# A Mamba scan with a routed FFN on one core: eight softplus sums on TensorE, other small work divided anew between VectorE and GpSimd, and a shorter routing chain

## What is computed

```python
xn = layernorm(x)
# attention part: layernorm again, then two Mamba blocks, one forward, one on the reversed sequence
xi, z = split(xn2 @ in_w.T);  xi = silu(conv4(xi) + conv_b)          # 256 inner features
dt, B, C = split(xi @ x_w.T)                                          # 8, 16, 16
delta = softplus(dt @ dt_w.T + dt_b)
h[t] = h[t-1] * exp(delta[t] * A) + (delta[t] * xi[t]) * B[t]         # 256 x 16 states
y[t] = sum_n h[t] * C[t] + xi[t] * D;   out = (y * silu(z)) @ out_w.T
attn = concat(out_f, out_b) @ combine_w.T + combine_b + xn
# FFN part: each token goes to one of 8 experts, argmax of xn @ router_w.T
ffn = down(silu(gate(xn)) * up(xn)) of that expert
result = x + attn + ffn
```

## Time and profile before

| | before |
|---|---|
| time, median of 3 runs (lowest to highest) | 910.14 us (907.42 to 910.88) |
| the profiled execution's own time | 907.48 us |
| its span, first to last instruction | 905.7 us |
| PE / DVE / ACT / POOL busy | 738.3 / 883.4 / 696.3 / 802.3 us |

### The profile page before, as it was taken

How to read it: one execution, slowest core, us unless ns; L and a number is a source line. 1 busy time by engine, 2 the same in 40 slices (tenths; PEclk the granted TensorE clock), 3 DMA queues, 4 the chain that set the end, 5 groups by cost and what they waited for, 6 DMA issues and landing times.

```text
span 905.7 us, 10749 instructions
## 1 busy us (share of the span) xinstructions
PE 738.3 (82%) x3033; PEld 329.6 (36%) x3033; DVE 883.4 (98%) x635; ACT 696.3 (77%) x1185; POOL 802.3 (89%) x453
## 2 busy tenths in 40 slices
PE   8889867886588988989797987989878879679376
PEld 5334312331134534444343533445333432224032
DVE  6999999999899999999999999999999999999997
ACT  5998864845479889988989989897979976575650
POOL 0788787999999999898899998999798999999996
PEclk8969797687799989999899999989989897988689
DMA  8894344134355555545455626455553444462400
GB/s 234 226 278 113 116 105 142 52 101 113 114 146 169 146 190 145 166 125 139 146 144 180 174 81 208 120 171 140 175 143 91 143 97 148 113 184 61 108 0 13
DMA packets 90988, 123.60 MB, mean 136 GB/s; under 512 B 7977, under 2 KB 63274, under 8 KB 86962
## 3 DMA queue, kind: packets, MB, share of 16 engines
q1 hardware_dynamic: 88882, 118.72, 46.5%
q0 software_dynamic: 2048, 4.20, 1.5%
HBM read 75.57 MB, written 14.29 MB: 99 GB/s over the span
## 4 chain that ended last, share of the span: by engine, by line
issue 39%; POOL 30%; PE 13%; ACT 9%; DVE 6%; DMA 1%; SPq 0%; ACTq 0%; POOLq 0%; DVEq 0%
POOL hs L1485 19%; POOL sorted_tokens L1496 4%; ACT dA L1032 3%; POOL gu_w L1458 3%; DVE hs L1245 2%; PE in_b L626 2%; DVE in_b L1226 2%; PE y L660 2%; ACT L1041 2%; POOL tmpA L1418 2%; PE front L579 2%; PE front L619 2%; POOL du L1423 1%; DVE hs L1243 1%; POOL yg L1468 1%
## 5 line engine op out<-in xcount | busy, mean ns | idle before, releaser
L1485 POOL TENSOR_TENSOR hs<-hs,C_rep 128x1024 f32<-128x1024 f32 x250 | 585.4, 2362 | 45.8 <-DVE hs L1245 24.6
L1032 ACT ACTIVATE dA<-delta_rep,A_sb 128x511 f32<-128x511 f32 x512 | 335.3, 717 | 20.4 <-DMA delta_rep<-tmpA 16.3
L1226 DVE TENSOR_TENSOR in_b<-in_b,B_rep 128x1024 f32<-128x1024 f32 x256 | 301.2, 1225 | 3.3 <-PE in_b L626 2.1
L1245 DVE TENSOR_TENSOR_SCAN hs<-dA,in_b 128x1024 f32<-128x1024 f32 x128 | 286.0, 2276 | 5.4 <-PE y L660 5.1
L1243 DVE TENSOR_TENSOR_SCAN hs<-dA,in_b 128x1024 f32<-128x1024 f32 x128 | 285.6, 2274 | 0.9 <-PE y L660 0.9
L626 PE MATMUL in_b<-du,cst 128*128 128x512 f32 x256 | 162.4, 721 | 60.9 <-DVE hs L1245 43.7
L660 PE MATMUL y<-hs,cst 128*32 128x512 f32 x1016 | 136.4, 655 | 22.1 <-POOL hs L1485 22.1
L579 PE MATMUL front<-xpad,w_in 128*128 128x512 f32 x248 | 117.4, 608 | 7.2 <-ACT xi L961 5.6
L1041 ACT ACT_TABLE_LOAD x71 | 91.1, 1283 | 11.6 <-PE moe L809 7.1
L626 PEld LDWEIGHTS in_b<-du,cst 128*128 128x128 f32 x256 | 47.7, 216 | 134.4 <-issue 129.9
L579 PEld LDWEIGHTS front<-xpad,w_in 128*128 128x128 f32 x248 | 46.2, 195 | 63.2 <-issue 49.8
(11 more groups left out here) (166 smaller groups left out, 810.7 us busy)
## 6 DMA issues: line engine op xcount, KB each, us to landing
delta_rep<-tmpA SPq DMA_DIRECT2D x126, 256.0 KB, 3.9
C_rep<-dbc_scratch SPq DMA_DIRECT2D x16, 1024.0 KB, 7.3
B_rep<-dbc_scratch SPq DMA_DIRECT2D x15, 1024.0 KB, 5.2
gu_w<-in_gate_up SPq DMA_DIRECT2D x39, 384.0 KB, 3.8
dn_w<-in_down SPq DMA_DIRECT2D x39, 192.0 KB, 2.6
xs<-sorted_tokens SPq DMA_DIRECT2D x39, 64.0 KB, 3.9
sorted_ffn<-ys SPq DMA_DIRECT2D x39, 64.0 KB, 2.4
sorted_tokens<-up_f SPq DMA_DIRECT2D x9, 256.0 KB, 4.5
```

What stands on the lines that cost most here:

```text
L1032: i = e.activation(dA[:, m % NA, r * L + 1:(r + 1) * L], src, ACT.Exp, scale=A_sb[:, d, 2 * p + jj, RH * rh + r:RH * rh + r + 1])
L1226: e.tensor_tensor(to, in_b[:, 2 + 2 * odd, :].unsqueeze(1).broadcast_to([P, RH, L]), by, ALU.mult).then_inc(dve_mult, 1)
L1245: e.tensor_tensor_scan(to[:, ::-1], a[:, 1:n + 1][:, ::-1], b[:, ::-1], 0.0, ALU.mult, ALU.add).then_inc(dve_scan, 1)
L1485: e.tensor_tensor(hs[:, m % NH, :], hs[:, m % NH, :], C_rep[:, u % 2, RH * rh:RH * rh + RH, :].rearrange("p r t -> p (r t)"), ALU.mult).th ...
```

## The change

- `SUM_STEP` names eight half-units, (3,0), (3,1), (4,0), (4,1), (14,0), (14,1), (15,0), (15,1). Their sum relu + ln is made by PE with two matmuls by the identity into bank `M` (`sum_delta`), at steps 41, 43, 57, 59, 218, 219, 232 and 235, and copied to `tmpA` by ACT one step later (`keep_delta`). POOL's addition is dropped there. SP's first `load_pair` of units 3 and 15 comes three steps later.
- `DU_STEP`: for unit 3 DVE multiplies delta, read from `M`, by xi (`first_du`), at steps 42 and 44; POOL does neither.
- `GATE_ON_DVE` gains i = 27 and 28. `C_ON_DVE` loses 41, 56, 180, 217 and 226 and keeps only the last, 255.
- The routing scans the one-hot before the matmuls instead of the counts behind them; one more matmul takes the place of a copy, a subtraction and an addition on DVE, the tile-to-expert table has one tile a partition (128x8 elements in place of 39x8 on each), and parts are packed: 18 instructions in place of 21, `pos_u` ready at step 32 in place of 35. The scatters and the loads in front of them start two steps sooner (POOL from step 31, SP from step 30).
- The `final_mm` of batches 2, 4 and 5 and the first transpose of the tiles wait for the copies out of `M`.

```diff
-GATE_ON_DVE = (3, 4, 5, 2 * UNITS - 1)
-C_ON_DVE = (41, 56, 180, 217, 226, LAST - 1)
+GATE_ON_DVE = (3, 4, 5, 27, 28, 2 * UNITS - 1)
+C_ON_DVE = (LAST - 1,)
+DU_STEP = {(3, 0): 42, (3, 1): 44}
+SUM_STEP = {(3, 0): 41, (3, 1): 43, (4, 0): 57, (4, 1): 59,
+            (UNITS - 2, 0): 218, (UNITS - 2, 1): 219, (UNITS - 1, 0): 232, (UNITS - 1, 1): 235}
...
                 for v in fronts(m, -5, -8):
-                    load_pair(v, 0)
+                    if (v, 0) not in SUM_STEP or v % 2 == 0:
+                        load_pair(v, 0)
+                for v in fronts(m, -5, -5):
+                    if (v, 0) in SUM_STEP and v % 2:
+                        load_pair(v, 0)
...
-                    if R0 + 5 + 20 * c // 8 == m:
+                    if R0 + 3 + 20 * c // 8 == m:
...
+            def sum_delta(v, h):
+
+                e.wait_ge(act_log, 2 * v + h + 1)
+                if (v, h) == (3, 0):
+                    e.wait_ge(dve_route, N_POS)
+                elif (v, h) == (UNITS - 2, 0):
+                    e.wait_ge(act_fin, 2)
+                elif v == UNITS - 1:
+                    e.wait_ge(act_fin, 4 + h)
+                if sums_on_pe(v, h) > 1:
+                    e.wait_ge(act_delta, sums_on_pe(v, h) - 1)
+                if 1 < sums_on_pe(v, h) <= 1 + len(DU_STEP):
+                    e.wait_ge(dve_du, sums_on_pe(v, h))
+                e.matmul(M[:, :], ident, tmpA[:, h, :], start=True, stop=False)
+                e.matmul(M[:, :], ident, tmpB[:, h, :], start=False, stop=True).then_inc(pe_delta, 1)
...
+                if b == 2:
+                    e.wait_ge(act_delta, sums_on_pe(UNITS - 2, 1))
+                if b >= 4:
+                    e.wait_ge(act_delta, sums_on_pe(UNITS - 1, b - 4))
...
+                for v, h in SUM_STEP:
+                    if SUM_STEP[v, h] == m:
+                        sum_delta(v, h)
...
-                if m == R0 + 3:
+                if m == R0 + 2:
                     e.wait_ge(dve_route, N_ONE)
-                    e.matmul(M[:, 0:256], tri, scratch(0), start=True, stop=True)
-                    e.matmul(M[:, 256:512], ones[:, :], scratch(0), start=True, stop=True).then_inc(pe_route, 1)
+                    upto = scratch(1)
+                    e.matmul(M[:, 256:256 + E], ones[:, :], upto[:, NBLK - 1::NBLK], start=True, stop=True)
+                    e.matmul(M[:, 0:256], ones[:, :], upto, start=True, stop=False)
+                    e.matmul(M[:, 0:256], tri, scratch(0), start=False, stop=True).then_inc(pe_route, 1)
...
+            def keep_delta(v, h):
+                e.wait_ge(pe_delta, sums_on_pe(v, h))
+                e.copy(tmpA[:, h, :], M[:, :]).then_inc(act_delta, 1)
...
+                for v, h in SUM_STEP:
+                    if SUM_STEP[v, h] + 1 == m:
+                        keep_delta(v, h)
...
+            def first_du(v, h):
+
+                wait_delta(e, v, h)
+                e.wait_ge(act_xi, 2 * v + h + 1)
+                e.wait_ge(pe_du, J * (v - 1 - h) + 4 + 4 * h)
+                e.tensor_tensor(du[:, du_slot(v, h), :], M[:, :], xi[:, v % 2, h, :], ALU.mult).then_inc(dve_du, 1)
...
+                elif part == 3:
+                    e.wait_ge(dve_route, 5)
+                    e.tensor_tensor_scan(upto, notfirst, one, 0.0, ALU.mult, ALU.add).then_inc(dve_route, 1)
...
-                elif part == 7:
-                    e.wait_ge(pe_route, 1)
-                    e.tensor_copy(val, M[:, 256:512]).then_inc(dve_route, 1)
...
-                    e.tensor_tensor(
-                        te.rearrange("p (n e) -> p n e", e=E), end_p.unsqueeze(1).broadcast_to([P, NTILE, E]),
-                        cst[:, C_TILE:C_TILE + NTILE].unsqueeze(2).broadcast_to([P, NTILE, E]),
-                        ALU.is_le).then_inc(dve_route, 1)
...
+                    e.tensor_scalar(te, end_p, cst[:, C_TILE:C_TILE + 1], None, ALU.is_le).then_inc(dve_route, 1)
...
             def delta_du(v, h):
-                e.wait_ge(act_log, 2 * v + h + 1)
-                e.tensor_tensor(tmpA[:, h, :], tmpA[:, h, :], tmpB[:, h, :], ALU.add).then_inc(pool_delta, 1)
+                if (v, h) not in SUM_STEP:
+                    e.wait_ge(act_log, 2 * v + h + 1)
+                    e.tensor_tensor(tmpA[:, h, :], tmpA[:, h, :], tmpB[:, h, :], ALU.add).then_inc(pool_delta, 1)
...
-                        if R0 + 6 + (20 * c + 5 * k) // 8 == m:
+                        if R0 + 4 + (20 * c + 5 * k) // 8 == m:
```

More of the change, by code:

```diff
@@ L134, in c_on_dve, with sums_on_pe, du_on_dve, du_on_pool @@
     return sum(x <= m for x in C_ON_DVE)
+def sums_on_pe(v, h):
+    return sum(k <= (v, h) for k in SUM_STEP)
+def du_on_dve(v, h):
+    return 1 + sum(k <= (v, h) for k in DU_STEP)
+def du_on_pool(v, h):
+    return 2 * v + h + 1 - du_on_dve(v, h)
+def sums_on_pool(v, h):
+    return 2 * v + h - sums_on_pe(v, h)
 def mamba_moe_kernel(nc, x, in_wT, conv_wT, x_wT, dt_wT, A_log, out_w, comb_wT, comb_b,
@@ L319, in wait_du @@
         def wait_du(e, v, h):
-            if v == 0 and h == 0:
-                e.wait_ge(dve_du, 1)
+            if v == 0 and h == 0 or (v, h) in DU_STEP:
+                e.wait_ge(dve_du, du_on_dve(v, h))
             else:
-                e.wait_ge(pool_du, 2 * v + h)
+                e.wait_ge(pool_du, du_on_pool(v, h))
         def wait_gated(e, i):
@@ L1273, in route @@
             def route(part):
-                one, val, pref, tmp = (scratch(i) for i in range(4))
-                rank, cum = M[:, 0:256], M[:, 256:512]
-                ntile, end_p, first, end = M[:, 0:E], M[:, E:2 * E], M[:, 2 * E:3 * E], small[:, 0:E]
-                te = th_f[:, :, :].rearrange("p a c -> p (a c)")[:, 0:NTILE * E]
+                one, upto, pos, tmp = (scratch(i) for i in range(4))
+                rank, notfirst = M[:, 0:256], M[:, 256:512]
+                total, ntile = M[:, 256:256 + E], M[:, 256 + E:256 + 2 * E]
+                first, end_p = small[:, E:2 * E], M[:, 256 + 2 * E:256 + 3 * E]
                 ke, ek = "p (k e) -> p k e", "p (e k) -> p e k"
-                best, low = small[:, 0:32], small[:, 32:64]
+                best, low, end, te = small[:, 0:32], small[:, 32:64], small[:, 0:E], tmp[:, E:2 * E]
                 if part == 0:
@@ L1310, in route @@
                     e.wait_ge(dve_route, 8)
[L1311 to L1314 removed]
+                    e.tensor_tensor_scan(end, ones[:, 0:E], ntile, 0.0, ALU.mult, ALU.add).then_inc(dve_route, 1)
                     e.wait_ge(dve_route, 9)
[L1316 to L1322 removed]
@@ L1323, in route @@
                     e.tensor_tensor(first, end, ntile, ALU.subtract).then_inc(dve_route, 1)
                     e.tensor_copy(end_p, end).then_inc(dve_route, 1)
[L1325 to L1326 removed]
+                elif part == 8:
+                    e.wait_ge(dve_route, 11)
                     e.scalar_tensor_tensor(
[L1328 to L1347 removed]
@@ new lines, in route @@
+                        rank.rearrange(ek, e=E), first.unsqueeze(2).broadcast_to([P, E, NBLK]), float(P),
+                        rank.rearrange(ek, e=E), ALU.mult, ALU.add).then_inc(dve_route, 1)
+                    e.wait_ge(dve_route, 12)
+                    e.tensor_tensor(pos, rank, one, ALU.mult).then_inc(dve_route, 1)
+                elif part == 9:
+                    e.wait_ge(dve_route, 13)
+                    e.tensor_reduce(low, pos.rearrange("p (e k) -> p k e", e=E), AX_X, ALU.add).then_inc(dve_route, 1)
+                    e.tensor_scalar(te, end_p, cst[:, C_TILE:C_TILE + 1], None, ALU.is_le).then_inc(dve_route, 1)
+                elif part == 10:
+                    e.wait_ge(dve_route, 15)
+                    e.tensor_copy(pos_u[:, :], low).then_inc(dve_route, 1)
+                    e.tensor_reduce(tmp[:, 0:1], te, AX_X, ALU.add).then_inc(dve_route, 1)
+                elif part == 11:
+                    e.wait_ge(dve_route, 17)
+                    e.tensor_scalar(ej_i[:, :], tmp[:, 0:1], float(E - 1), None, ALU.min).then_inc(dve_route, 1)
@@ L1397, in vector_program @@
                         gate(i)
+                for v, h in DU_STEP:
+                    if DU_STEP[v, h] == m:
+                        first_du(v, h)
                 if m == LAST + 5:
@@ L1478, in gpsimd_program @@
                     for v in fronts(m, (-7, -4)[h], (-8, -6)[h]):
-                        delta_du(v, h)
+                        if (v, h) not in DU_STEP:
+                            delta_du(v, h)
                 if m < LAST and m not in C_ON_DVE:
@@ L1513, in shape_constants @@
     c[:, C_ID:C_ID + P] = np.eye(P)
-    c[:, C_TRI:C_TRI + P] = np.triu(np.ones((P, P)), 1)
+    c[:, C_TRI:C_TRI + P] = np.triu(np.ones((P, P)), 1) - 1.0
     c[:, C_SEL:C_SEL + DD] = np.repeat(np.eye(DD), G, axis=0)
```

73 lines of the change are left out of this document (25 added, 48 removed).

## The result

| | before | after |
|---|---|---|
| median (lowest to highest, runs) | 910.51 us (907.42 to 913.84, 4) | 900.59 us (896.49 to 901.36, 4) |
| ratio, 95% interval | | 0.9882 [0.9845, 0.9919] |
| the profiled execution, its span | 907.48, 905.7 | 899.89, 898.0 |

A forecast was written before the change was run, and what follows sets the result against it. DVE, busy 98% of the span, was taken as the bound, with its stalls. Terms of -6.8 us before stretch two and -1.2 in it gave -8.0, taking the median from 910.1 to 902.1 us; 8-in-10 range 897.5 to 906.5.

The forecast's parts named there:

- stretch one: Scatters, steps 31 to 61: POOL, relieved of work, ends C(54) at 232.9, so PE can begin 8.4 us sooner.
- C(56) and C(180): C products of steps 56 and 180 leave DVE's program: -1.1 us each.
- the `first_du`: Two products of delta and xi for unit 3, added to DVE's program at 0.6 us each: +1.2 us.
- the routing: Fewer and smaller routing instructions on DVE: -1.2 us, between -0.8 and -1.6.
- the stall at scan 61: DVE's stall of 3.06 us at the end of the scatters goes, as C(54) ends sooner: -3.1 us.
- The waits of unit 3: DVE waits at unit 3 for PE's added sums and the work queued behind them: +1.2 us (0 to 3).
- the log comes at about 174.8 and the sum at 177.4: Unit 3's second sum on PE: z's projection stands behind the first sum, its copy ready at 178 to 180.
- Rival (a): PE's sums are mostly hidden, unit 3 costs 0 and stretch two gives 3: -11.3, 899 us; chance 0.24.
- So the 2.04 and 0.86 at 861 go: DVE's two stalls around step 245 vanish because C(238) ends 3.5 us sooner relative to the stretch's start: -2.9 us.
- The term of stretch two: Gathers, steps 206 to 245: 2.9 us gained less 1.7 lost by scan 238: -1.2 us (gain 0 to 3).
- rival (b): Stalls return at 61 and 238, PE's longer queue eating up POOL's relief: -3.0, 907 us; chance 0.13.
- C(41) -3.0: C product of step 41 leaves DVE: 3.0 us, some 1.1 to 1.2 its work and 1.9 blocking by POOL.

The follow-up runs named there:

- e12_same: The changed kernel run once more with nothing edited: 897.92 us, ratio 0.9875, span 894.4.
- e9_c41: The changed kernel with the C product of step 41 back on DVE: one execution, 900.24 us, span 898.5.
- e3_route: The kernel before with only the new routing and earlier scatters, all six C products on DVE: 921.86 us, ratio 1.0106.
- e2_two: The changed kernel with C products 41, 56 and 180 back on DVE, additions and products of units 3 and 4 on POOL: 913.58 us, ratio 1.0049.
- e10_order: The changed kernel with filler matmuls in PE's pauses, step 244's bias, residual and last w_out matmul one step later, final_mm behind sum_states: 897.44 us, ratio 0.9845.
- e1_one: The changed kernel with the sums of units 14 and 15, gates 27 and 28 and C products 217 and 226 as before: 902.63 us, ratio 0.9908.
- e7_pool151: The changed kernel with the sum of (15,1) added by POOL as before: 900.76 us, ratio 0.99.

## Why the prediction was right, and where it was not

**Right, with its reason.** The limit was DVE's program plus few stalls, and in stretch one the account holds term by term: C(56) and C(180) 1.1 each, the `first_du` 0.6 each, the routing -0.9 (near the weaker bound; I took -1.2), the stall at scan 61 gone with C(54) at 230.4. The queue of POOL, counted product by product and scatter by scatter, was 0.1 us off after 93 us.

**The waits of unit 3: +1.2, measured 0.** The failed step is "the log comes at about 174.8 and the sum at 177.4". z's projection was done at 170.1 and the log at 173.1, 1.7 us earlier, and the sum's two matmuls took 1.13 and 1.02, at the high clock; the sum ended at 175.1, its copy at 175.8, and the spread that I put at 186 to 188 ended at 182.5. (0.9 us of this DVE shares, which came to `first_du` (3,1) at 177.8 and not 178.7, since this execution left the start-up sooner; in e12_same it left later, and the waits are 0 as well.) I had chained z's projection behind the first sum as if each began where my estimate ended, and the mean clock of the stretch rose from 0.78 to 0.87, which I had held at its old value. Rival (a) was right for this place.

**"So the 2.04 and 0.86 at 861 go": wrong as a statement.** I asked when POOL delivers C(238), not when PE is done with what follows. The step left out is PE's queue behind the release, `sum_states`, bias, residual, spread: 9.8 us at the low clock and 7.0 us with the clock rising after the first. In one execution the stall is 2.8 us, in another 0. The term of stretch two, -1.2 with bounds 0 to -3, measured -0.5 and -3.5. I had that clock in rival (b) as 1.8 us a sum; it acts on all that stands on the path, not on the added sums alone.

**"C(41) -3.0": the size was right and the owner wrong.** 1.8 of it is a block that goes with the scatters' move (e9_c41, e3_route).

**The sum as a sum: the largest flaw, and the result hides it.** I took nine terms as independent. They are not: routing and scatters alone cost 11 us and not -1.2 (e3_route), C(56) on DVE takes 13.2 us from scan to scan and not 1.1 once the scatters are early (e3_route, e2_two), and the sums and `first_du` are worth 7.8 us in that frame, at scans 53 to 76, where before had a stall at scan 61 alone. The routing, booked at -1.2, makes the largest loss; the sums with `first_du`, booked at +2.7, mend a good part of it. The total is right because the change contains both, and that is luck as far as the working goes. So is a part of the close agreement in the table: the start-up (-1.0) and the small stalls (+2.2) had no term, the waits at unit 3 and at 57 and 59 (+1.5) did not come, and these nearly cancel. The second execution of the same program gives -11.2, and all eight runs have the median 899.1; that is the -11.3 and 899 of rival (a). The prediction had asked of each moved step which queue it goes past; it asked it of POOL up to C(54) and not of C(46), the first that the early scatters delay, nor of the DVE product that had been sheltered by them.

**Gate 28.** The longer wait was foreseen, its cause not: 1.24 of it is `final_mm` (e10_order), and e1_one, which has neither the sum at step 235 nor the gate, has the same 1.24 before scan 238. At most 0.33 is the sum's (e7_pool151), and that is not shown, as the same wait is 0.42 in e12_same and 1.19 in e1_one.

**Open.** Why the clock rises when it does was not tested; nor how C(56) is let in after 12 us. That it enters in the gap of 0.07 us that POOL has between the addition and the dependent product (240.67 to 240.74) is argued from the ends of the two records, 241.75 and 242.87, not shown.

## What to carry to other kernels

When a change moves work earlier on one engine and takes work off the same engine elsewhere, price the parts jointly: walk the queue of that engine past every consumer between the two places, the first delayed one above all, and ask which instructions of other engines had been running in gaps that the move closes. A stall is gone only when all that stands between its release and its consumer is done in time, at the lower of the engine's two clocks. And before a difference of a few microseconds is explained by an edit, profile the same program twice.
